# A lambda-layer bottleneck in 32 images: v's transfers on ScalarE's queue, other tiles and copies on VectorE, sums and first outputs in another order

## Chip, cores and metric

One core of a Trainium2 chip runs the whole program. The metric is the device time of one execution in microseconds (us). The engines are TensorE (PE: matrix products), VectorE (DVE), ScalarE (ACT), GpSimd (POOL) and SyncE (SP). Each works through its own instructions in order, and semaphores order them against each other. SP and ACT also issue DMA transfers, from queues of their own. An x of 32 images with 512 channels of 64x64 points comes from DRAM in float32, and the output goes back there.

## What is computed

The reference, cut to what matters, with `x` an image of 512 channels:

```python
n = group_norm(x)                          # 32 groups of 16 channels
h = relu(bn1(conv1x1(n, w1)))              # 512 -> 128 channels
q = bnq(conv1x1(h, wq))                    # 64 = 4 heads x 16
k = softmax(conv1x1(h, wk), axis=channels) # 16
v = bnv(conv1x1(h, wv))                    # 32
pos = conv2d(v, emb, 15x15, "same")        # for each of 16 k and 32 v
content = k @ v.T                          # 16 x 32
lam = q . content + q . pos                # 128 channels
h = relu(bn2(lam))
out = x + relu(bn3(conv1x1(h, w3)) + n)    # 128 -> 512 channels
```

## The kernel before

The image loop is software-pipelined. One trip of it has two stages. The stage `lam` computes image b's lambda from q and v, and takes image b+1's group statistics beside it. The stage `mixed` (the list `MIX`) then works on two images in turn: the last convolution and output of image b, and the projections c (conv1), q and k/v of image b+1. A prologue (`PRO`) and an end (`END`) do the same for the first and the last image. Pixels are cut into four chunks of 1024; `c0` to `c3`, `q0` to `q3` and `k0` to `k3` are the chunks' matmul groups, `o<j>.<t>` is the output tile of chunk j and channel block t (tile n = 4j+t, 128x1024), `nb` a small bias product, `cl` and `cp` the content lambda, `w<u>.<s>` a slot of the convolution's weights (it becomes the moving operand of `lam`), and `r0`, `r1` their rest.

**The order.** TensorE runs `MIX` exactly as `mix_names` lists it. Each group is written into one of four PSUM buffers, ring0 to ring3. The buffer is `n % 4` of a running count (`placed`); o3.t take ring2 and ring3 by turns, and the weights ring0 and ring1. A group waits until the one before it in its buffer has been read out (`take`, `moved`). The other engines go through the same list in order.

**c, q, k.** ACT turns c's PSUM into h1 (L779) and issues the reload of x for the output (L781, its only DMAs). For q, ACT writes a bfloat16 part (L787) and DVE the remainder r1 (L970). For k, DVE copies k out, writes v, takes the maximum and subtracts it (L977 to L983). ACT casts r1 (L791), spreads v over three copies (`spread_v`, L728 to L730) and takes the exponential of k (`softmax_exp`, L720). `softmax_sum` on DVE (L954 to L956) waits for that exponential, sums, takes the reciprocal and multiplies: it normalizes k. In the kernel before it runs for chunk j-1 behind k's work of chunk j, and for chunk 3 right behind that. POOL makes the third part of q (`split_q`, L1164).

**v's way.** After k3, `store_v` writes v to DRAM in three window transfers and a rest (L365, L368), and `load_v` reads it back in the layout of the convolution (L375, L376). Both are issued by SP, in one program with q's stores (L351, L352), q's loads (L358, six a chunk), the output's stores (L400) and the next image's x (L343). `cl` waits for all four normalized chunks (`soft_ready`), `w0.0` for all of q's loads (`q_in`), `lam` for v's.

**Output.** A tile in `VEC_TILES` takes two DVE passes (L1019, L1022). A tile in `POOL_TILES` takes one DVE pass into S (L1015), a ReLU on ACT (L735, `relu_half`, one place later) and an addition on POOL (L1171). `bn2_relu` on ACT (L715) must have made chunk j of h2 before o<j>.<t>.

**The lead.** The first unit of weights, w0.0 to w0.7, r0 and r1, closes `MIX`. `BY_DVE` names the slots that DVE copies out of PSUM (L696 on both engines); ACT copies the rest.

Of the kernel before, what the change touches and what calls it, by code (L numbers as in the profile page):

```python
# [12 lines left out]
P = 128  # L13
# [3 lines left out]
PAD = (R - 1) // 2  # L17
# [10 lines left out]
BLK = 8  # L28
WROWS = 21
WCOLS = 22  # L30
TROWS = 6 * WROWS
# [7 lines left out]

BY_DVE = {0: (1, 5), 1: (1, 3), 2: (3,), 3: (3,), 4: (3,), 5: (1, 3, 5, 7)}  # L40
ACT_SLOTS = [(u, s) for u in range(UNITS) for s in range(NS) if s not in BY_DVE[u]]
# [4 lines left out]

VEC_TILES = [0, 2, 3, 5, 7, 8, 10, 12, 13, 15]
POOL_TILES = [n for n in range(16) if n not in VEC_TILES]
# [12 lines left out]
def mix_names():  # L61
    order = ["c0", "nb", "c1", "q0", "k0", "o0.0", "o0.1", "c2", "q1", "k1", "o0.2", "o0.3", "c3", "q2", "k2", "q3", "k3",
             "o1.0", "o1.1", "o1.2", "o1.3", "cl", "o2.0", "cp", "o2.1", "o2.2", "o2.3"]
    lead = lead_names()
    for t in range(4):
        order += [f"o3.{t}", lead[t]]
    return order + lead[4:]
# [25 lines left out]
def lambda_block(nc, x, w1, bn1, wq, bnq, wk, wv, bnv, emb, bn2, w3, bn3, out):  # L93
# [9 lines left out]
    NCH = N // CHUNK  # L103
# [15 lines left out]
    with ctx:  # L119
# [221 lines left out]
        def _(sp):  # L341
# [18 lines left out]

            def store_v(im):
                sp.wait_ge(vpad_ready, im * 3 + 3)
                sp.wait_ge(vx_ready, im * (3 * NCH) + 3 * NCH)
                for a, n in ((0, 8), (8, 8), (16, 5)):
                    sp.dma_start(vD[PAD:PAD + W, a:a + n, :],  # L365
                                 vX[:, 0:n, a // BLK:a // BLK + NYB, :].rearrange("x r m v -> x r (m v)"))\
                        .then_inc(v_out, 16)
                sp.dma_start(vR[PAD:PAD + W, :], vX[:, 5, 2:2 + NYB, :].rearrange("x m v -> x (m v)"))\  # L368
                    .then_inc(v_out, 16)

            def load_v(im):
                sp.wait_ge(v_out, im * 64 + 64)
                for t in range(3):
                    src = bass.AP(vD.tensor, t * TROWS * ROW, [[ROW, P], [BLK * WROWS * ROW, NXB], [1, ROW]])
                    sp.dma_start(V[:, t, :, :], src).then_inc(v_in[t], 16)  # L375
                sp.dma_start(Vrem, bass.AP(vR.tensor, 0, [[ROW, WCOLS], [BLK * ROW, NXB], [1, ROW]])).then_inc(vrem_in, 16)  # L376

            def load_v3(b):
# [56 lines left out]
            for j in range(NCH):  # L435
                store_q(0, j)
                load_q(0, j)
            store_v(0)
            load_v(0)

# [9 lines left out]
            with nc.Fori(0, B - 1, engines=OrderedEngineSet([sp.engine]), hint_back_edge=True) as b:  # L450
                lam(b, False)
                store_q(b + 1, 0)
                load_q(b + 1, 0)
                store_out(b, 0)
                store_out(b, 1)
                store_q(b + 1, 1)
                load_q(b + 1, 1)
                store_out(b, 2)
                store_q(b + 1, 2)
                store_out(b, 3)  # L460
                load_q(b + 1, 2)
                store_q(b + 1, 3)
                store_v(b + 1)
                load_q(b + 1, 3)
                load_v(b + 1)
                for n in range(4, 16):
                    store_out(b, n)
# [241 lines left out]
        def _(act):  # L709
            def bn2_relu(b, j):  # L710
# [4 lines left out]
                nc.scalar.activation(part, part, ACT.Relu, bias=pbi[:, 1:2], scale=psc[:, 1:2]).then_inc(h2_ready, 1)  # L715

            def softmax_exp(im, j):
                cols = slice(j * (CHUNK // P), (j + 1) * (CHUNK // P))
                act.wait_ge(kmax_done, im * NCH + j + 1)
                nc.scalar.activation(kS[:, cols, :], kS[:, cols, :], ACT.Exp).then_inc(kexp_done, 1)  # L720
# [49 lines left out]
            def front(name, at, im, with_reload):  # L770
# [18 lines left out]
                else:  # L789
                    act.wait_ge(r1_ready, im * NCH + j + 1)  # L790
                    nc.scalar.copy(q12[:, 0, j * CHUNK:(j + 1) * CHUNK], r1[:, j % 2, :]).then_inc(qm_done, 1)  # L791
                    spread_v(im, j)
                    softmax_exp(im, j)

# [15 lines left out]
            act.wait_ge(setup_vd, 8 * 16)  # L810
            for name in PRO:
                if name[0] in "wr":
                    lead(name, AT_PRO, 0)
                elif name[0] in "cqk" and name[1] in "0123":
                    front(name, AT_PRO, 0, False)
            with nc.Fori(0, B - 1, engines=OrderedEngineSet([act.engine]), hint_back_edge=True) as b:
                lam(b, True)
                late = []
                for name in MIX:
# [6 lines left out]
                    late = []  # L826
                    if name == "c0":
                        bn2_relu(b, 0)
                        bn2_relu(b, 1)
                    if name == "k0":  # L830
                        bn2_relu(b, 2)
                        bn2_relu(b, 3)
                    if name[0] == "o" and int(name[1]) * CT + int(name[3:]) in POOL_TILES:
# [10 lines left out]
        def _(dve):  # L844
# [113 lines left out]
            def front(chain, name, at, im):  # L958
                kind, j = name[0], int(name[1])
                src = ring[at[name]]  # L960
                if kind == "q":
                    dve.wait_ge(q_full, im * NCH + j + 1)
                    dve.wait_ge(qh_ready, im * NCH + j + 1)
# [9 lines left out]
                elif kind == "k":  # L973
# [9 lines left out]
                    nc.vector.tensor_tensor(k, k, spread, ALU.subtract).then_inc(kmax_done, 1)  # L983
                    if j:
                        softmax_sum(chain, im, j - 1)

# [243 lines left out]
```

## Time and profile before

| | us |
|---|---|
| median of 3 runs | 5176.27 |
| lowest, highest | 5169.3, 5177.41 |
| the profiled execution | 5191.58 |
| its span, first to last instruction | 5188.9 |

The profile is of one execution. Its page gives each engine's busy time and groups of instructions; further views of the same trace list waits, instructions in order of time, the chain of work that ended last, and stretches with the granted TensorE clock. Times within the trace are from the span's start. Idle time in brackets stands ahead of an instruction, with what released it. All stretches below are of one trip of the loop in the middle of the run, whose `nb` products stand at 2604.07.

### The profile page before, as it was taken

The page shows a single profiled execution, that of the slowest core. Times are in us where ns is not written, and L with a number is a line of the kernel's source. Part 1 is how long each engine was busy: PE and PEld are TensorE (multiplying, and loading weights), DVE is VectorE, ACT ScalarE, POOL GpSimd, SP SyncE. Part 2 cuts the span into 40 slices and gives each one's busy share as a digit, 9 for nine tenths or more (in the row PEclk, how much of TensorE's full clock was granted, in tenths as well). Part 3 has the DMA queues.
Part 4 walks back from the last instruction along what each step waited for, and adds up shares of the span by engine and source line. Part 5 has one row for each costly group of instructions (what it writes and reads, how often), then busy time and mean ns, then how long its engine had stood idle before and what let it go on. Part 6 is the DMA issues. An engine that isn't in the chain of part 4 may idle for free.

```text
span 5188.9 us, 120753 instructions
## 1 busy us (share of the span) xinstructions
PE 4668.3 (90%) x49366; PEld 2754.3 (53%) x49366; DVE 2959.6 (57%) x4695; ACT 2285.5 (44%) x2816; POOL 748.1 (14%) x433
## 2 busy tenths in 40 slices
PE   4989999998999999999989998999988999999997
PEld 2555555554555555555545555555555555555554
DVE  4456555565555565655655555655556565566564
ACT  1444445444444444444444444444444444444443
POOL 0011110111111111101111111111011111111111
PEclk8899999899999989999899989899999999998998
DMA  3678767778777787677787777876777867778776
GB/s 96 224 241 292 261 215 257 245 259 292 231 236 253 252 281 266 217 249 248 257 290 234 232 256 246 287 261 210 256 249 260 289 226 236 248 253 290 254 221 227
DMA packets 537170, 1284.13 MB, mean 247 GB/s; under 512 B 43048, under 2 KB 225324, under 8 KB 528556
## 3 DMA queue, kind: packets, MB, share of 16 engines
q1 hardware_dynamic: 471276, 1017.22, 60.1%
q10 hardware_dynamic: 65472, 260.05, 13.5%
q8 instruction: 415, 6.80, 0.6%
q14 instruction: 7, 0.06, 0.0%
HBM read 844.79 MB, written 432.33 MB: 246 GB/s over the span
## 4 chain that ended last, share of the span: by engine, by line
PE 63%; issue 11%; DVE 9%; DMA 5%; SPq 4%; ACT 4%; POOL 3%; ACTq 0%; DVEq 0%; POOLq 0%
PE ring L522 16%; PE ring L503 14%; PE ring L648 13%; PE ring L578 7%; PE ring L602 4%; DMA X<-x_dram 3%; PE ring L529 3%; POOL X L1171 2%; PE ring L534 2%; PE ring L612 2%; SPq L358 2%; DVE S L1015 2%; ACT region L696 1%; DVE region L696 1%; DMA q_parts<-region 1%
## 5 line engine op out<-in xcount | busy, mean ns | idle before, releaser
L696 ACT COPY region<-ring 126x1024 f32<-126x1024 f32 x1184 | 1163.9, 1016 | 1157.0 <-PE ring L503 1147.8
L578 PE MATMUL ring<-h,w3T 128*128 128x512 f32 x2048 | 1015.6, 639 | 108.4 <-DVE S L1015 76.7
L503 PE MATMUL ring<-Qt,Ep 96*126 96x256 bf16 x5120 | 855.7, 309 | 112.5 <-ACT region L696 62.8
L522 PE MATMUL ring<-X,w1e 128*128 128x512 f32 x2048 | 907.8, 596 | 28.8 <-DVE w1e L892 28.8
L648 PE MATMUL ring<-region,V 126*32 126x128 f32 x24576 | 879.9, 288 | 24.9 <-issue 24.7
L503 PEld LDWEIGHTS ring<-Qt,Ep 96*126 96x126 bf16 x5120 | 628.9, 153 | 358.8 <-issue 181.8
L648 PEld LDWEIGHTS ring<-region,V 126*32 126x32 f32 x24576 | 678.6, 115 | 246.9 <-issue 236.1
L696 DVE COPY region<-ring 126x1024 f32<-126x1024 f32 x352 | 430.3, 1222 | 646.7 <-PE ring L503 646.7
L868 DVE BATCH_NORM_STATS2 st<-X 128x6 f32<-128x512 f32 x1024 | 624.7, 680 | 199.2 <-DMA X<-x_dram 199.1
L578 PEld LDWEIGHTS ring<-h,w3T 128*128 128x128 f32 x2048 | 388.5, 201 | 536.1 <-issue 387.6
L522 PEld LDWEIGHTS ring<-X,w1e 128*128 128x128 f32 x2048 | 385.0, 191 | 496.3 <-issue 493.0
L1171 POOL TENSOR_TENSOR X<-X,S 128x1024 f32<-128x1024 f32 x192 | 451.3, 2351 | 1014.4 <-ACT S L735 1014.4
L970 DVE SCALAR_TENSOR_TENSOR region<-ring,pbi,region 64x512 f32<-64x512 f32 x256 | 179.4, 739 | 708.0 <-ACT region L787 706.9
L1019 DVE SCALAR_TENSOR_TENSOR ring<-X,r1cur,ring 128x1024 f32<-128x1024 f32 x320 | 410.9, 1284 | 138.0 <-PE ring L578 136.9
L735 ACT ACTIVATE S<-S,bcur 128x1024 f32<-128x1024 f32 x192 | 220.1, 1147 | 545.1 <-DVE S L1015 545.1
L1164 POOL TENSOR_TENSOR region<-region 64x1024 bf16<-64x1024 f32 x128 | 272.9, 2132 | 1200.6 <-ACT region L791 1200.6
L779 ACT ACTIVATE region<-ring,nb 128x1024 f32<-128x1024 f32 x128 | 141.9, 1109 | 645.5 <-PE ring L522 344.6
L1022 DVE SCALAR_TENSOR_TENSOR X<-ring,bcur,X 128x1024 f32<-128x1024 f32 x320 | 410.9, 1284 | 11.3
L1157 POOL MEMSET region<- 64x224 f32 x32 | 13.1, 411 | 2220.0 <-PE ring L648 2176.2
L534 PEld LDWEIGHTS ring<-wkvT,region 128*128 128x128 f32 x2048 | 238.2, 191 | 103.9 <-issue 77.9
L534 PE MATMUL ring<-wkvT,region 128*128 128x48 f32 x2048 | 254.1, 277 | 0.0
L1015 DVE SCALAR_TENSOR_TENSOR S<-X,rcur,ring 128x1024 f32<-128x1024 f32 x192 | 244.6, 1274 | 5.5 <-PE ring L578 5.2
(127 smaller groups left out, 2980.1 us busy)
## 6 DMA issues: line engine op xcount, KB each, us to landing
X<-x_dram SPq DMA_DIRECT2D x132, 2048.0 KB, 21.0
out_dram<-X SPq DMA_DIRECT2D x512, 512.0 KB, 9.8
X<-x_dram ACTq DMA_DIRECT2D x124, 2048.0 KB, 9.8
Qt<-q_parts SPq DMA_DIRECT2D x768, 128.0 KB, 3.0
V<-v_windows SPq DMA_DIRECT2D x96, 1024.0 KB, 8.1
lambda_sums<-S SPq DMA_DIRECT2D x64, 1024.0 KB, 3.9
h<-lambda_sums SPq DMA_DIRECT2D x256, 256.0 KB, 5.2
q_parts<-region SPq DMA_DIRECT2D x128, 256.0 KB, 4.1
```

What stands on the lines that cost most here:

```text
L503: last = nc.tensor.matmul(dst[0:TROWS, i * 256:(i + 1) * 256], taps(u, xo, yo), Q[:, :, xo * BLK + yo, :], start=(i % 2 == 0), stop=True, ...
L522: last = nc.tensor.matmul(dst[:, hh * HALF:(hh + 1) * HALF], w1e[:, c, :], X[:, j, c, hh * HALF:(hh + 1) * HALF], start=(c == 0), stop=(c ...
L534: last = nc.tensor.matmul(dst[:, i * KV:(i + 1) * KV], h1[:, j % 2, i * P:(i + 1) * P], wkvT[:, :], start=True, stop=True)
L578: last = nc.tensor.matmul(dst[:, yb * HALF:(yb + 1) * HALF], w3T[:, t, :], src, start=True, stop=True)
L648: last = nc.tensor.matmul(bank_of(i)[c * DV:(c + 1) * DV, (g % 4) * P:(g % 4 + 1) * P], V[0:TROWS, VSLOT[t], xb, yb * DV:(yb + 1) * DV], W ...
L696: return engine_copy(dst, src)
L868: return nc.vector.bn_stats(st[:, c, 2 * j + hh, :], X[:, j, c, hh * HALF:(hh + 1) * HALF])
L1015: nc.vector.scalar_tensor_tensor(T[:, i % 2, :], X[:, j, t, :], rcur[:, t:t + 1], src[:, :], ALU.mult, ALU.add).then_inc(half_sum, 1)
L1019: nc.vector.scalar_tensor_tensor(src[:, :], X[:, j, t, :], r1cur[:, t:t + 1], src[:, :], ALU.mult, ALU.add).then_inc(whole_sum, 1)
L1022: nc.vector.scalar_tensor_tensor(X[:, j, t, :], src[:, :], bcur[:, t:t + 1], X[:, j, t, :], ALU.add, ALU.max).then_inc(out_ready, 1)
L1164: nc.gpsimd.tensor_tensor(q12[:, 1, cols], r1[:, j % 2, :], q12[:, 0, cols], ALU.subtract)\
L1171: nc.gpsimd.tensor_tensor(X[:, j, t, :], X[:, j, t, :], T[:, i % 2, :], ALU.add).then_inc(pool_out, 1)
```

## The change

1. `store_v` and `load_v` move from SP's program to ACT's. The stores are issued in k3's work, between `spread_v` and `softmax_exp`; the loads at o1.2 (in the prologue at w0.0). SP's list closes over the gap, and its output stores come one place later, o1.0 (tile 4) ahead of q's last loads.
2. `VEC_TILES` goes from 10 tiles to 12, so `POOL_TILES` goes from 1, 4, 6, 9, 11, 14 to 5, 7, 9, 11.
3. Of the lead, DVE copies w0.5 and w0.7, where it copied w0.1 and w0.5.
4. `softmax_sum` of chunk j-1 stands ahead of q<j>'s work on DVE, where it stood behind k<j>'s. The last one stays behind k3.
5. o0.0 and o0.1 come behind k1 (before: k0), o0.2 and o0.3 behind c3 (before: k1). `bn2_relu` of the four chunks goes behind k0, k1, q2 and q3 (before: two behind c0, two behind k0).

```diff
-BY_DVE = {0: (1, 5), 1: (1, 3), 2: (3,), 3: (3,), 4: (3,), 5: (1, 3, 5, 7)}
+BY_DVE = {0: (5, 7), 1: (1, 3), 2: (3,), 3: (3,), 4: (3,), 5: (1, 3, 5, 7)}
-VEC_TILES = [0, 2, 3, 5, 7, 8, 10, 12, 13, 15]
+VEC_TILES = [0, 1, 2, 3, 4, 6, 8, 10, 12, 13, 14, 15]
...
-    order = ["c0", "nb", "c1", "q0", "k0", "o0.0", "o0.1", "c2", "q1", "k1", "o0.2", "o0.3", "c3", "q2", "k2", "q3", "k3",
+    order = ["c0", "nb", "c1", "q0", "k0", "c2", "q1", "k1", "o0.0", "o0.1", "c3", "o0.2", "o0.3", "q2", "k2", "q3", "k3",
...
+            def store_v(im):
+                act.wait_ge(vpad_ready, im * 3 + 3)
+                act.wait_ge(vx_ready, im * (3 * NCH) + 3 * NCH)
+                for a, n in ((0, 8), (8, 8), (16, 5)):
+                    act.dma_start(vD[PAD:PAD + W, a:a + n, :],
...
                     spread_v(im, j)
+                    if j == NCH - 1:
+                        store_v(im)
                     softmax_exp(im, j)
...
+                    if name == "o1.2":
+                        load_v(b + 1)
-                    if name == "c0":
+                    if name == "k0":
                         bn2_relu(b, 0)
+                    if name == "k1":
                         bn2_relu(b, 1)
-                    if name == "k0":
+                    if name == "q2":
                         bn2_relu(b, 2)
+                    if name == "q3":
                         bn2_relu(b, 3)
...
                 if kind == "q":
+                    if j:
+                        softmax_sum(chain, im, j - 1)
                     dve.wait_ge(q_full, im * NCH + j + 1)
...
-                    if j:
-                        softmax_sum(chain, im, j - 1)
```

ACT, in the loop, at k3: the cast, the three copies of v and the exponential of the kernel before. In both kernels kS is k, region holds v's copies and q's parts, and S the halves of POOL's tiles.

```order
L791 CAST region<-region 64x1024
L728 COPY region<-region 64x4x64
L729 COPY region<-region 64x3x64
L730 COPY region<-region 64x64
L720 ACTIVATE kS<-kS 128x128
L734 REGISTER_ALU
L735 ACTIVATE S<-S,bcur 128x1024
```

ACT, the same place in the changed kernel.

```order
L788 CAST region<-region 64x1024
L725 COPY region<-region 64x4x64
L726 COPY region<-region 64x3x64
L727 COPY region<-region 64x64
L698 ISA
L699 ISA
L701 DMA v_windows<-region 64x8x256 x2
L701 DMA v_windows<-region 64x5x256
L704 DMA v_rest<-region 64x256
L717 ACTIVATE kS<-kS 128x128
```

Two waits and four transfers now stand between v's copies and k3's exponential, and the exponential's own row is otherwise unchanged.

DVE, in the loop, the end of tile 3 and the start of q2 and k2 in the kernel before (ring3 is tile 3's buffer, ring1 q2's).

```order
L1022 SCALAR_TENSOR_TENSOR X<-ring3,bcur,X 128x1024
L962 REGISTER_ALU
L970 SCALAR_TENSOR_TENSOR region<-ring1,pbi,region 64x64x8 x2
L977 COPY kS<-ring2 128x128
```

DVE, the same place in the changed kernel: tile 3 (ring0), then the sum of chunk 1, then q2.

```order
L1024 SCALAR_TENSOR_TENSOR ring0<-X,r1cur,ring0 128x1024
L1026 REGISTER_ALU
L1027 SCALAR_TENSOR_TENSOR X<-ring0,bcur,X 128x1024
L959 TENSOR_REDUCE kst<-kS 128x8
L859 REGISTER_ALU
L960 RECIPROCAL kst<-kst 128x8
L859 REGISTER_ALU
L961 TENSOR_TENSOR kS<-kS,kst 128x128
L969 REGISTER_ALU
L977 SCALAR_TENSOR_TENSOR region<-ring1,pbi,region 64x64x8 x2
```

The three instructions of chunk 1's sum moved from behind k2 to ahead of q2, and tile 3's two passes come straight before them, since their matmuls moved behind c3.

## Rows read from the trace of the kernel before

**Rows 1.** The page: busy time, share of the span and instructions of each engine.

```profile
PE 4668.3 (90%) x49366; PEld 2754.3 (53%) x49366; DVE 2959.6 (57%) x4695; ACT 2285.5 (44%) x2816; POOL 748.1 (14%) x433
```

**Rows 2.** Waits of PE: who waited for whom, us in total, times, longest.

```profile
PE ring L578 <- DVE S L1015: 76.7, 31, 3.0
PE ring L612 <- issue: 68.8, 35, 2.4
PE ring L554 <- DVE Qt L991: 63.2, 32, 2.0
...
PE ring L648 <- issue: 24.7, 14, 3.4
```

**Rows 3.** PE in order of time: start, us, line, count, [idle before <- releaser].

```profile
2640.22 1.93 PE L529 MATMUL ring<-region,wqT 128*64 128x512 f32 x4
...
2647.68 7.10 PE L578 MATMUL ring<-h,w3T 128*128 128x512 f32 x16
...
2661.78 0.34 PE L554 MATMUL ring<-Qt 16*96 16x32 f32 x2 [2.03 <-DVE Qt L991]
...
2671.34 2.54 PE L578 MATMUL ring<-h,w3T 128*128 128x512 f32 x4 [2.17 <-DVE S L1015]
2675.14 1.11 PE L503 MATMUL ring<-Qt,Ep 96*126 96x256 bf16 x4 [1.25 <-DMA Qt<-q_parts]
2676.04 3.59 PE L578 MATMUL ring<-h,w3T 128*128 128x512 f32 x4
```

**Rows 4.** DVE in order of time, from tile 3 to tile 11.

```profile
2638.16 1.28 DVE L1022 SCALAR_TENSOR_TENSOR X<-ring,bcur,X 128x1024 f32<-128x1024 f32 x1
2643.53 1.40 DVE L970 SCALAR_TENSOR_TENSOR region<-ring,pbi,region 64x512 f32<-64x512 f32 x2 [4.09 <-ACT region L787]
...
2651.58 1.66 DVE L956 TENSOR_TENSOR kS<-kS,kst 128x128 f32<-128x128 f32 x1
...
2653.71 0.29 DVE L956 TENSOR_TENSOR kS<-kS,kst 128x128 f32<-128x128 f32 x1
2653.92 1.27 DVE L1015 SCALAR_TENSOR_TENSOR S<-X,rcur,ring 128x1024 f32<-128x1024 f32 x1
...
2670.01 1.27 DVE L1015 SCALAR_TENSOR_TENSOR S<-X,rcur,ring 128x1024 f32<-128x1024 f32 x1
```

**Rows 5.** ACT at q3 and k3, in order of time.

```profile
2647.08 1.24 ACT L787 ACTIVATE region<-ring,pbi 64x512 bf16<-64x512 f32 x2
2649.84 1.04 ACT L791 CAST region<-region 64x1024 bf16<-64x1024 f32 x1 [1.53 <-DVE region L970]
...
2651.74 0.30 ACT L720 ACTIVATE kS<-kS 128x128 f32<-128x128 f32 x1
```

**Rows 6.** POOL's `split_q` of chunk 3, in order of time.

```profile
2650.96 2.13 POOL L1164 TENSOR_TENSOR region<-region 64x1024 bf16<-64x1024 f32 x1 [2.74 <-ACT region L791]
```

**Rows 7.** SP in order of time: issue start, us, line, what is transferred, count.

```profile
2661.66 3.71 SPq L365 DMA_DIRECT2D v_windows<-region  x3
2665.42 2.50 SPq L368 DMA_DIRECT2D v_rest<-region  x1
2667.97 4.82 SPq L358 DMA_DIRECT2D Qt<-q_parts  x6
```

**Rows 8.** Issues of L365 and L368: ns min/median/max, first and last start.

```profile
L365 SPq DMA_DIRECT2D v_windows<-region x96: 587/660/2389, 138.6 to 5040.6; - x96
...
L368 SPq DMA_DIRECT2D v_rest<-region x32: 2291/2468/2517, 142.1 to 5042.9; - x32
```

**Rows 9.** The chain that ended last, ACT's queue at c2: start, us, what.

```profile
2626.31 0.38 ACTq L781
...
2626.73 0.04 ACTq L734
```

**Rows 10.** Stretches: us, busy (x count) of PE, PEld, DVE, ACT, POOL, granted clock, DMA share, GB/s.

```profile
2550.00:2554.00 4.00, 3.86 (x54) 3.25 (x53) 4.00 (x7) 1.93 (x2) 0.00 (x0) 0.50 1.04 414
...
2674.00:2678.00 4.00, 2.87 (x7) 1.83 (x8) 2.49 (x2) 1.01 (x1) 0.89 (x1) 0.50 0.95 318
```

More of the change, by code:

```diff
@@ L359, in load_q @@
                         .then_inc(q_in[j], 16)
[L361 to L376, printed above, removed]
             def load_v3(b):
@@ L437, in _ @@
                 load_q(0, j)
-            store_v(0)
-            load_v(0)
             def lam(b, last):
@@ L453, in _ @@
                 load_q(b + 1, 0)
+                store_q(b + 1, 1)
+                load_q(b + 1, 1)
                 store_out(b, 0)
                 store_out(b, 1)
-                store_q(b + 1, 1)
-                load_q(b + 1, 1)
+                store_q(b + 1, 2)
                 store_out(b, 2)
-                store_q(b + 1, 2)
                 store_out(b, 3)
@@ L462, in _ @@
                 store_q(b + 1, 3)
-                store_v(b + 1)
+                store_out(b, 4)
                 load_q(b + 1, 3)
-                load_v(b + 1)
-                for n in range(4, 16):
+                for n in range(5, 16):
                     store_out(b, n)
@@ L715, in bn2_relu, with load_v @@
                 nc.scalar.activation(part, part, ACT.Relu, bias=pbi[:, 1:2], scale=psc[:, 1:2]).then_inc(h2_ready, 1)
+            def store_v(im):
[3 more added lines that the diff above has]
+                    act.dma_start(vD[PAD:PAD + W, a:a + n, :],
+                                 vX[:, 0:n, a // BLK:a // BLK + NYB, :].rearrange("x r m v -> x r (m v)"))\
+                        .then_inc(v_out, 16)
+                act.dma_start(vR[PAD:PAD + W, :], vX[:, 5, 2:2 + NYB, :].rearrange("x m v -> x (m v)"))\
+                    .then_inc(v_out, 16)
+            def load_v(im):
+                act.wait_ge(v_out, im * 64 + 64)
+                for t in range(3):
+                    src = bass.AP(vD.tensor, t * TROWS * ROW, [[ROW, P], [BLK * WROWS * ROW, NXB], [1, ROW]])
+                    act.dma_start(V[:, t, :, :], src).then_inc(v_in[t], 16)
+                act.dma_start(Vrem, bass.AP(vR.tensor, 0, [[ROW, WCOLS], [BLK * ROW, NXB], [1, ROW]])).then_inc(vrem_in, 16)
             def softmax_exp(im, j):
@@ L811, in _ @@
             for name in PRO:
+                if name == "w0.0":
+                    load_v(0)
                 if name[0] in "wr":
```

## The prediction, made before the changed kernel was run

> **What bounds the kernel now.** I read the page first, then PE's waits, then one trip of the loop in order of time on PE, DVE, ACT, POOL and SP. PE is busy for 90% of the span, DVE for 57%, ACT for 44% [rows 1]. PE is the bound in most of a trip, and an edit pays only where PE waits. Its largest waits come once a trip (31 times each), for DVE in the middle of `mixed` and for nothing that the profile shows in `lam` [rows 2]. In the trip shown PE works without a gap through c, q, k and o1.0 to o1.3, until 2654.8 [rows 3]. Then it waits for DVE, above all ahead of cp (2.03 us) and of o3.0 (2.17 us, for tile 11's pass to free the buffer) [rows 3]. DVE itself has no real pause from q2's pass at 2643.53 to the end of tile 11's pass at 2671.28 [rows 4]. So this stretch is DVE's, every us of delay in it reaches o3.0, and behind that the lead and `lam`.
>
> **The change, part by part**, for one trip, in the times of that trip.
>
> *Outputs one place later.* PE's work up to o1.3 keeps its sum and has no gap, so q2 still starts at 2640.22 [rows 3]. A full-speed tile takes 7.10/4 = 1.78 us of PE [rows 3], so tile 2's matmuls now end at about 2638.5. DVE's two passes for tiles 2 and 3 (four by 1.28 us) end at 2643.6, where they ended at 2639.44 and left DVE idle for 4.09 us [rows 4]. The cover is gone. With chunk 1's sum (0.8 us) ahead of it, q2's pass starts at 2644.4 and not at 2643.53: +0.9 us. `bn2_relu` sits in ACT's pauses.
>
> *Sums ahead of q.* The multiply of a sum takes 0.29 us alone, but 1.66 where POOL's `split_q` runs, and ends 0.15 us behind POOL [rows 4, 6]. Behind k2 and k3 it met POOL; chunks 0 and 1 now don't. Chunk 2's sum must wait for its exponential, which ACT reaches 0.9 us later than before, right ahead of q3's ACT part [rows 5]. So q3's pass on DVE stays 0.9 us late. Behind k3 there is one sum less on DVE, but the last waits for k3's exponential (now ending 0.95 us later than 2652.04) and then for POOL (3.09 becomes 4.0). It ends at 2654.3, and tile 4's pass begins 0.4 us later than before, if nothing else stands in ACT's way. These two edits together: +0.4 us. Bounds: -0.7 (no delay at q2) to +0.9 (all of it stays).
>
> *v's transfers on ACT.* The stores stand ahead of k3's exponential. SP needs 3.71 us to issue the three window stores and 2.50 for the rest, 6.2 us from 2661.66 to 2667.92 [rows 7]; over the whole run the medians are 0.66 and 2.47 [rows 8]; with two windows at 0.66, the third at 2.2 (here 3.71 less 1.32 is 2.4), the four make 6.0. That this is not SP's backlog alone shows in the least value for the rest, 2291 ns, over all 32 images, the first with its idle queues among them [rows 8]. ACT's own issue of x, 0.38 us, is followed by its next queue instruction only behind its end [rows 9], so I take the exponential to be held for the sum. Bounds: four at the least window value, 0.59, is 2.4 us; with the greatest, 2.39, for each window store and 2.52 for the rest it is 9.7. I take 6.0, since the same four transfers take it on the other queue. The exponential then ends at 2659.0, not 2653.0, and chunk 3's sum (0.8 us, with no `split_q` beside it any more) at 2659.8. Before, tile 4's pass began at 2653.92 [rows 4]. That is +5.9 us, with the delays of the two edits above already in it, and nothing hides it: DVE has tile 4 behind that sum, and cl waits for the sum too. PE has run out of work by 2654.8.
>
> *Tiles.* From tile 4 to tile 11 both kernels have four two-pass tiles and four half tiles (4 and 6 change places with 5 and 7). The 17.4 us from 2653.92 to 2671.28 [rows 4] shrink by the 0.3 us or so that DVE waits for PE in it. In the tail tile 14 takes one more pass, 1.28, and w0.1's copy (1.2) leaves DVE; w0.7's copy joins it, while tile 14's ReLU leaves ACT, where it stood ahead of w0.3's copy. I put the tail at 0, between -0.5 and +1.3. The loads of v on ACT stand ahead of tile 7's ReLU (5.7 us of issue, about 2661 to 2667), whose result POOL and DVE need by tile 11 at 2675: covered by some 5 us.
>
> *SP without v.* q's last loads came behind v's stores [rows 7] and held w0.0 for 1.25 us [rows 3]; they now land well before w0.0. The output stores go out earlier as well, and the next x with them, so the 16 DMA engines, at a share of 1.0 and above through the start of `lam` [rows 10], finish earlier against PE. The wait at L648 with no cause in the profile (24.7 us over the run [rows 2]) came at the end of that full stretch in part of the images. I take -1.0 us for both. Bounds: 0, and -6, if the wait at L612 (2.2 us a trip [rows 2]) and the slow clock behind it also went.
>
> The Trainium skill says of this (DMA: Bandwidth & Descriptors, section "Issuing engines are not separate DMA queues") that transfers from several engines share the same 16 DMA engines, and that a second issuer saves only issue time, "usually small relative to the DMA itself". The first half speaks against a gain in bandwidth; the second doesn't fit v's rest, with 2.47 us of issue for 64 KB.
>
> *The clock.* At 0.50 of the clock (1.2 GHz) a tile's matmuls take 3.59 us, not 1.78 [rows 3, 10]. That stretch came behind the waits ahead of o3.0. Now PE idles some 6 us longer from 2654.8, so I expect more time at 1.2 GHz in o2 and o3. DVE needs 5.1 us for tiles 9 to 11, PE 10.7 for three at 1.2 GHz: if all three fall in it, the trip loses about 3.5 us more, with o3.0 and o3.1 too about 8. If none do, 0. I take +1.5, nearer to none, since PE idles in this stretch anyway.
>
> **Sum.** A trip: 5.9 + 1.5 - 1.0 - 0.3 = +6.1 us; 31 trips: +189. The prologue hides the stores (w0.0 waits there for q's loads), and in the end DVE has two more passes of 1.28, with POOL's last one gone: +2. Together +191. The profiled execution would go from 5191.6 to 5383. The median before is 15 us below it, and the change falls on it alike: 5176.3 + 191 = 5367 us, 3.7% slower.
>
> **The rivals.**
> *The issue is cheap on ACT.* Its queue is idle by then, and 0.38 us for x of 2 MB speaks for it; the least value of the rest, 2.29, against. At 2.4 us for the four, the last sum ends at 2656.2: a trip is 2.3 + 0.5 for the clock - 1.3 = +1.5; 31 by 1.5 + 2 = +49, 5225 us. Chance 0.12.
> *The exponential isn't held (ends faster).* If ACT can start it while the issues run, only +0.4 is left, against -1.0 for SP and DMA, -0.3 for DVE's waits and -0.4 for the clock: -1.3 a trip, 31 by -1.3 + 2 = -38, 5138 us. The point is whether an ACT instruction can begin during an issue that stands ahead of it. No row shows one that does [rows 9]. Chance 0.07. Here the Trainium skill has a rule (Advanced Engine Details and Errata, "Sequencer Loop"): while a control instruction executes, other engine instructions can be read and queued. If issues count as such, this rival holds; no row here shows it.
> *The waits in `lam` go.* With x landing earlier against PE, L612's wait and its slow stretch fall away: -5 a trip more than the forecast, 31 by 1.1 + 2: 5212 us. For it: the wait comes only once a trip, at one place, with the DMA engines full. Against: the DMA traffic still follows tile 15 and reaches over that place. Chance 0.06.
> *The clock falls through o3.* 3.5 to 7 us more a trip than the forecast: 31 by 9.6 + 2 is 5476 us, 31 by 13.1 + 2 is 5584. Chance 0.07.
>
> **Chances.** Forecast 0.66; the rest as above, and 0.02 for no difference. The forecast's own spread is that of the issue (4.5 to 7) and of the clock (0 to 3.5): 31 by 3.1 to 31 by 9.1, 5274 to 5460 us. The range reaches from the cheap issue to there: 5225 to 5460. A difference under about 0.2% (10 us) can't be told from none. Faster 0.08, within it 0.04, slower 0.88.
>
> **What would show it.** ACT: four issues of together about 6 us between v's last copy and k3's exponential. DVE: an idle time of about 7 us (k3's work ends at 2651.9) ahead of the last sum (L959), put down to ACT's exponential. PE: a wait of about 7 us ahead of cl (its buffer is tile 4's, whose two passes end at 2662.3), none for q's loads. The sums' multiplies of chunks 0 and 1 at 0.29 us. o3.0 some 73 us behind `nb`, not 67. The prediction is wrong if that idle time isn't there, or if `lam` becomes shorter by several us.

## The result: 7.1% slower, about twice the loss forecast

| | before | changed |
|---|---|---|
| median, us | 5175.89 | 5539.74 (4 runs, 5528.28 to 5555.31) |
| ratio, 95% interval | 1 | 1.0708 [1.0679, 1.0736] |
| span of the profiled execution | 5188.9 | 5541.3 |
| mean granted clock of TensorE | 0.923 | 0.891 |
| one trip, mean of 31 (`nb` to `nb`) | 157.9 | 168.9 |

The forecast was 5367 us, in a range of 5225 to 5460. The direction was right. The time lies 173 us above the forecast and 80 above the range. A trip became 10.9 us longer, where +6.1 was forecast. 31 trips make 339 of the 352 us by which the span grew.

The page of the changed kernel, which answers to [rows 1], has the same matmuls in a longer span. PE's busy time grew by 40 us, so most of the loss is idle time. In its chain of work the bare "issue" has 13% and ACT's queue 4%:

```profile
PE 4708.6 (85%) x49366; PEld 2811.2 (51%) x49366; DVE 2931.6 (53%) x4759; ACT 2221.8 (40%) x2752; POOL 597.1 (11%) x369
...
PE 61%; DVE 13%; issue 13%; ACT 5%; ACTq 4%; POOL 3%; SPq 1%; DMA 0%; DVEq 0%; POOLq 0%
```

Waits of the changed kernel on PE, DVE and ACT (who waited for whom, us in total, times, longest), against [rows 2]. L530 is cl, L558 the output convolution, L592 the wait in `lam` that stood at L612:

```profile
PE ring L530 <- DVE X L1027: 262.2, 31, 8.6
PE ring L558 <- DVE S L1020: 214.5, 31, 10.2
PE ring L592 <- issue: 92.0, 40, 4.1
...
DVE kst L959 <- ACT kS L717: 354.0, 97, 7.9
...
DVE S L1020 <- POOL X L1176: 114.4, 27, 6.9
...
ACT S L732 <- issue: 322.7, 28, 14.1
...
ACT kS L717 <- issue: 211.9, 32, 6.8
```

There are two new stalls, one in every trip and one in 27 of the 31, and each can be followed through the engines. The first is the one forecast: the exponential (L717) is held for 6.6 us a time, DVE's last sum waits for it, and PE's cl waits 8.5 us for tile 4's passes. The second isn't in the forecast: a ReLU (L732) is held for 11.5 us a time (28 times), POOL's addition (L1176) waits for that, DVE's pass of tile 11 (L1020) for POOL, and PE's o3.0 for DVE, 6.9 us a trip where [rows 2] has 2.5.

ACT in one trip (its `nb` stands at 2599.82), in order of time, against [rows 5]. L701 and L704 are v's stores, L711 and L712 v's loads:

```profile
2648.60 4.24 ACTq L701 DMA_DIRECT2D v_windows<-region  x3
2652.87 2.32 ACTq L704 DMA_DIRECT2D v_rest<-region  x1
2655.24 0.31 ACT L717 ACTIVATE kS<-kS 128x128 f32<-128x128 f32 x1 [6.67 <-issue]
2660.17 1.15 ACT L732 ACTIVATE S<-S,bcur 128x1024 f32<-128x1024 f32 x1 [4.63 <-DVE S L1020]
2660.25 6.88 ACTq L711 DMA_DIRECT2D V<-v_windows  x3
2667.16 8.16 ACTq L712 DMA_DIRECT2D Qt<-v_rest  x1
2675.44 2.19 ACT L732 ACTIVATE S<-S,bcur 128x1024 f32<-128x1024 f32 x2 [14.12 <-issue]
```

The row at 2655.24 is the forecast's first step. The last three rows are the step that failed: the loads' issue takes 15.0 us here, and the ReLUs of tiles 7 and 9 come together behind it. The same place on DVE, POOL and PE, against [rows 4] and [rows 3]:

```profile
2655.58 0.29 DVE L959 TENSOR_REDUCE kst<-kS 128x8 f32<-128x128 f32 x1 [7.73 <-ACT kS L717]
...
2656.14 0.29 DVE L961 TENSOR_TENSOR kS<-kS,kst 128x128 f32<-128x128 f32 x1
...
2670.84 1.28 DVE L1027 SCALAR_TENSOR_TENSOR X<-ring,bcur,X 128x1024 f32<-128x1024 f32 x1
2679.04 1.28 DVE L1020 SCALAR_TENSOR_TENSOR S<-X,rcur,ring 128x1024 f32<-128x1024 f32 x1 [6.92 <-POOL X L1176]
```

```profile
2676.66 4.66 POOL L1176 TENSOR_TENSOR X<-X,S 128x1024 f32<-128x1024 f32 x2 [12.84 <-ACT S L732]
```

```profile
2659.01 3.59 PE L530 MATMUL ring<-region,kS 128*16 128x32 f32 x64 [8.48 <-DVE X L1027]
...
2680.38 3.37 PE L558 MATMUL ring<-h,w3T 128*128 128x512 f32 x4 [10.15 <-DVE S L1020]
```

The margin can be read off these rows. DVE was free for tile 11 at 2672.1. To have tile 7's half out of S by then, POOL (2.35 us) had to begin at 2669.8 and the ReLU (1.15) at 2668.6. The loads began at 2660.25. So a string of issues of up to 8.3 us costs nothing here, and the string of 15.0 us came 6.8 us too late for that; DVE waited 6.92.

SP at the same time, against [rows 7], and then the group of all its issues of q's loads (min/median/max in ns). The six loads of q's chunk 2 take 1.5 us each beside ACT's stores, where the median over the run is 0.6:

```profile
2648.99 9.01 SPq L358 DMA_DIRECT2D Qt<-q_parts  x6
...
L358 SPq DMA_DIRECT2D Qt<-q_parts x768: 578/597/2312, 105.8 to 5388.2; - x192
```

Over all trips the stores' issue takes 6.5 us and the loads' 12.2 (the mean, from 60.4 to 72.7 us behind `nb`). The groups of the loads' issues (min/median/max in ns) are of that size by their medians, 3 by 1.98 and 7.37, together 13.3:

```profile
L711 ACTq DMA_DIRECT2D V<-v_windows x96: 387/1984/4601, 137.0 to 5384.2; - x96
...
L712 ACTq DMA_DIRECT2D Qt<-v_rest x32: 2375/7368/8521, 140.5 to 5387.4; - x32
```

### The profile page after: what moved, and what is told of

Read it like the earlier page. It is cut to its first block, busy times and chain, and to the rows that moved or that the text cites. A ratio compares the mean times of both kernels' runs of the same rounds, so it can differ in the third digit from the quotient of the medians.

```text
span 5541.3 us, 120502 instructions
## 1 busy us (share of the span) xinstructions
PE 4708.6 (85%) x49366; PEld 2811.2 (51%) x49366; DVE 2931.6 (53%) x4759; ACT 2221.8 (40%) x2752; POOL 597.1 (11%) x369
## 4 chain that ended last, share of the span: by engine, by line
PE 61%; DVE 13%; issue 13%; ACT 5%; ACTq 4%; POOL 3%; SPq 1%; DMA 0%; DVEq 0%; POOLq 0%
PE ring L502 16%; PE ring L483 14%; PE ring L628 13%; PE ring L558 6%; DVE ring L1024 5%; PE ring L582 4%; POOL X L1176 2%; ACTq L701 2%; PE ring L514 2%; PE ring L509 2%; PE ring L592 2%; DVE S L1020 1%; DVE region L676 1%; ACTq L704 1%; DVE region L977 1%
## 5 line engine op out<-in xcount | busy, mean ns | idle before, releaser
L558 PE MATMUL ring<-h,w3T 128*128 128x512 f32 x2048 | 1022.0, 642 | 232.4 <-DVE S L1020 214.5
L558 PEld LDWEIGHTS ring<-h,w3T 128*128 128x128 f32 x2048 | 396.6, 205 | 673.4 <-issue 398.5
L1024 DVE SCALAR_TENSOR_TENSOR ring<-X,r1cur,ring 128x1024 f32<-128x1024 f32 x384 | 492.9, 1284 | 320.2 <-PE ring L558 319.5
L1027 DVE SCALAR_TENSOR_TENSOR X<-ring,bcur,X 128x1024 f32<-128x1024 f32 x384 | 493.1, 1284 | 13.7
L1176 POOL TENSOR_TENSOR X<-X,S 128x1024 f32<-128x1024 f32 x128 | 299.6, 2350 | 798.2 <-ACT S L732 798.2
L732 ACT ACTIVATE S<-S,bcur 128x1024 f32<-128x1024 f32 x128 | 143.8, 1144 | 601.1 <-issue 322.7
L530 PE MATMUL ring<-region,kS 128*16 128x32 f32 x2048 | 113.2, 240 | 273.5 <-DVE X L1027 262.2
L530 PEld LDWEIGHTS ring<-region,kS 128*16 128x16 f32 x2048 | 108.3, 129 | 299.3 <-DVE X L1027 287.9
```

Source lines behind the costliest of these rows:

```text
L558: last = nc.tensor.matmul(dst[:, yb * HALF:(yb + 1) * HALF], w3T[:, t, :], src, start=True, stop=True)
L1024: nc.vector.scalar_tensor_tensor(src[:, :], X[:, j, t, :], r1cur[:, t:t + 1], src[:, :], ALU.mult, ALU.add).then_inc(whole_sum, 1)
L1027: nc.vector.scalar_tensor_tensor(X[:, j, t, :], src[:, :], bcur[:, t:t + 1], X[:, j, t, :], ALU.add, ALU.max).then_inc(out_ready, 1)
L1176: nc.gpsimd.tensor_tensor(X[:, j, t, :], X[:, j, t, :], T[:, i % 2, :], ALU.add).then_inc(pool_out, 1)
```

## The experiments

The kernels start from the changed one, but for the one headed as part 1 alone. Ratios are against the kernel before, run beside it on the same chip. A trip is the mean from `nb` to `nb` over 31 stretches, of which the first holds the end of the prologue in place of a `mixed`. Each is read from one profiled execution, so differences of a few tenths are not told from none.

### v's transfers back on SP

Parts 2 to 5 are left as they are; only part 1 is undone. In the diff the lines taken out are ACT's, the ones put in SP's.

```diff
-                    if j == NCH - 1:
-                        store_v(im)
...
-                    if name == "o1.2":
-                        load_v(b + 1)
...
                 store_q(b + 1, 3)
-                store_out(b, 4)
+                store_v(b + 1)
                 load_q(b + 1, 3)
+                load_v(b + 1)
+                store_out(b, 4)
```

> The changed kernel with v's stores and loads issued by SP again, at the places of the kernel before (stores ahead of q's last loads, loads behind them); tiles, lead copies, sums and output order stay changed. Theory A (all the loss comes from ACT's two strings of issues, the stores ahead of k3's exponential and the loads ahead of tile 7's ReLU): within 20 us of the kernel before, 5176. Theory B (the output order, the two more double-pass tiles and DVE's copies of w0.5 and w0.7 carry a good part): 5250 or more.

Measured: 5160.67 us, ratio 0.9992 [0.9975, 1.0008], a trip of 157.1 us: theory A. The whole loss goes with part 1. Parts 2 to 5 neither cost nor gain by themselves: cl now waits 2.0 us (0.5 before) and o3.0 3.2 (2.5 before), cp a little less, and the mean clock is 0.936.

### One of the two holds at a time

The stores are put behind the exponential (loads still on ACT, ahead of tile 7's ReLU):

```diff
                     spread_v(im, j)
+                    softmax_exp(im, j)
                     if j == NCH - 1:
                         store_v(im)
-                    softmax_exp(im, j)
```

> The changed kernel with ACT issuing v's stores behind k3's exponential and not ahead of it. The loads stay at o1.2, ahead of tile 7's ReLU. Theory A1 (the two holds add up: 6 us for the stores, 4 to 5 for the loads): 6 us a trip less, about 5350. Theory A2 (they overlap, since the loads can't start before the stores have landed, some 60 us behind nb, and then hold tile 7's ReLU, and through POOL DVE's tile 11, until about 73 us behind nb whatever came before): only about 1 us a trip less, 5500 to 5530, with DVE's wait ahead of the last sum gone and its wait for POOL at tile 11 longer by as much.

Measured: 5528.02 us, ratio 1.071 [1.068, 1.0739], a trip of 168.1: theory A2. The wait at cl fell to 2.0 us, and next to none of it was gained. Waits of PE, DVE and ACT in this kernel:

```profile
PE ring L558 <- DVE S L1020: 427.8, 31, 17.2
...
PE ring L530 <- DVE X L1027: 63.1, 31, 2.0
...
DVE S L1020 <- POOL X L1176: 331.5, 31, 14.1
...
ACT S L732 <- issue: 696.1, 62, 19.1
```

o3.0 now waits 13.8 us a time: what cl waits less is there. Its time is set by the loads, and these can't start earlier: they wait for v's stores to land, some 60 us behind `nb` in both kernels.

The loads leave ACT for SP, behind q's last loads (stores still ahead of the exponential):

```diff
-                    if name == "o1.2":
-                        load_v(b + 1)
...
                 load_q(b + 1, 3)
+                load_v(b + 1)
```

> The changed kernel with v's loads issued by SP behind q's last loads; the stores stay on ACT ahead of k3's exponential. Theory A (the loads' issue on ACT is what the forecast had too small): the wait of DVE for POOL at tile 11 goes, the wait ahead of the last sum (7.7 us) stays: about 4.5 us a trip less than the changed kernel, 5380 to 5420, where the forecast of 5367 would have been near. Theory C (the excess is the clock: the 8 us of idle PE ahead of cl bring 1.2 GHz into o2 and o3): less than 1.5 us a trip back, 5490 or more.

Measured: 5414.08 us, ratio 1.0489 [1.0463, 1.0515], a trip of 164.7: theory A. Only the forecast's stall is left. L539 is cl here, L567 the output convolution, L957 DVE's sum, L719 the exponential. The page's first line, and waits:

```profile
PE 4674.6 (86%) x49366; PEld 2790.9 (52%) x49366; DVE 2929.4 (54%) x4759; ACT 2224.3 (41%) x2752; POOL 597.8 (11%) x369
...
PE ring L539 <- DVE X L1025: 260.4, 31, 8.7
...
PE ring L567 <- DVE S L1018: 97.6, 31, 3.2
...
DVE kst L957 <- ACT kS L719: 352.4, 97, 7.9
...
ACT kS L719 <- issue: 210.2, 32, 6.9
```

Both edits together:

> Both: ACT issues v's stores behind k3's exponential, SP issues v's loads behind q's last loads. Theory A: neither hold is left, so near the kernel before or below it, 5130 to 5190, since SP no longer spends 6 us on the stores ahead of q's last loads. Theory B (the other parts cost): 5250 or more.

Measured: 5169.55 us, ratio 0.9996 [0.9978, 1.0015], a trip of 157.2: theory A. ACT still issues the stores here, behind the exponential, and the ReLU behind them starts late (200.3 us over 31 times in this kernel's row of waits), but nobody waits for that. The page's first line, and waits:

```profile
PE 4592.8 (89%) x49366; PEld 2720.8 (53%) x49366; DVE 2946.8 (57%) x4759; ACT 2222.1 (43%) x2752; POOL 596.7 (12%) x369
...
PE ring L567 <- DVE S L1018: 101.2, 31, 3.7
PE ring L601 <- issue: 90.8, 49, 2.4
PE ring L539 <- DVE X L1025: 63.0, 31, 2.0
...
PE ring L637 <- issue: 40.5, 17, 4.4
...
ACT S L734 <- issue: 200.3, 31, 6.8
```

The four kernels make a square (us a trip):

| | loads on SP | loads on ACT |
|---|---|---|
| stores behind the exponential | 157.2 | 168.1 |
| stores ahead of it | 164.7 | 168.9 |

Stores alone +7.5, loads alone +10.9, both +11.7. The delays of the two holds run beside each other and end at the same place, o3.0, so they don't add.

### Part 1 alone, on the kernel before

> The kernel before with v's stores and loads issued by ACT, at the changed kernel's places; nothing else changed. Theory A (the two holds on ACT are the whole loss, about 11.5 us a trip by the runs with v on SP): 5500 to 5560. Theory B (the holds cost less without the changed tiles and order, since the output order or tile 7's place makes them bite): under 5450.

Measured: 5413.95 us, ratio 1.0473 [1.0447, 1.0498], a trip of 164.8, +6.8. Theory A of that text missed and B held. The loads take 7.8 us there, not 12.2, DVE waits next to nothing for POOL (3.7 us over the whole run, 114.4 in the changed kernel), and cl waits 5.3 us, not 8.5. So part 1 costs 6.8 us a trip on the kernel before, and 11.8 (168.9 less 157.1) on top of parts 2 to 5, though these cost nothing by themselves. What of them does it is the question of the last two experiments.

### The loads behind tile 7's ReLU

The stores are behind the exponential, and the loads come at cl, behind the ReLU that they held:

```diff
-                    if name == "o1.2":
+                    if name == "cl":
                         load_v(b + 1)
```

> The changed kernel with ACT's stores behind k3's exponential and ACT's loads at cl, behind tile 7's ReLU and not ahead of it; both strings of issues still run on ACT. Theory A (the loads cost through that one ReLU: POOL's addition of tile 7 is late, and DVE's pass for tile 11 waits for the buffer): against 5528 with the loads ahead of the ReLU some 9 to 11 us a trip come back, 5170 to 5240; what stays is that w0.0's and w0.1's copies wait for the end of the issues, about 74 us behind nb. Theory D (a string of 12 to 15 us of issues on ACT costs its length wherever it stands in mixed): 5400 or more.

Measured: 5387.09 us, ratio 1.043 [1.0408, 1.0451], a trip of 163.9, against 168.1 with the loads one place earlier: between the two theories. The stall at o3.0 went to 3.3 us, which shows that it was this one ReLU. But another stall came up, in all trips. PE's waits:

```profile
PE ring L483 <- DMA Qt<-q_parts: 168.0, 32, 17.7
...
PE ring L558 <- DVE S L1020: 103.6, 31, 3.6
```

w0.0 waits 4.9 us a trip for q's last loads, which land some 74 us behind `nb`, while v's loads are under way on the other queue. Slow issue on SP isn't the reason: these six loads take 3.9 us to issue, 3.8 with neither hold (means over the trips). But the last of them lands 6.6 us behind its issue, where it takes 2.3 with neither hold. So the time is lost behind the issue; whether to v's loads or to the output stores beside them isn't separated.

### SP kept quiet while ACT issues the loads

SP issues q's last loads only once most of V has landed:

```diff
                 store_out(b, 4)
+                sp.wait_ge(v_in[2], b * 16 + 32)
                 load_q(b + 1, 3)
```

> The changed kernel, and SP waits for the third of v's window loads to land before it issues q's last loads and the output stores behind them, so that ACT issues v's loads while SP issues nothing. It measures a duration, the time gets worse (w0.0 waits for q). Theory G (SP's issues and transfers beside it stretch ACT's string for v's loads, 12.2 us in the changed kernel against 5.6 on SP before): the string falls to 6 to 9 us. Theory H (ACT's queue issues these loads slower by itself): it stays at 11 or more.

Measured: 5599.43 us, ratio 1.0827 [1.0775, 1.0878], a trip of 170.4, since w0.0 now waits 4.5 us for q. What it was made for is the issue: the loads' string takes 8.2 us a trip, where it took 12.2, and the rest of v 2.7 us, where it took 6.7. That is theory G, but not the whole of the growth: the three window loads take 5.6 us here and 5.5 in the changed kernel, and 2.7 on SP in the kernel before. No run tells what makes the windows longer on ACT, so theory H isn't excluded for them. One trip of this kernel, ACT in order of time, and PE's waits:

```profile
2686.62 5.50 ACTq L712 DMA_DIRECT2D V<-v_windows  x3
2692.15 2.84 ACTq L713 DMA_DIRECT2D Qt<-v_rest  x1
2695.10 1.15 ACT L733 ACTIVATE S<-S,bcur 128x1024 f32<-128x1024 f32 x1 [7.41 <-issue]
```

```profile
PE ring L531 <- DVE X L1028: 261.2, 31, 8.7
PE ring L484 <- DMA Qt<-q_parts: 152.1, 32, 11.8
PE ring L559 <- DVE S L1021: 104.2, 31, 5.1
```

At 8.3 us in this trip the string is right at the margin worked out above, and the stall at o3.0 is 3.4 us a trip, as without any loads on ACT.

### The order of the outputs undone

Parts 1 to 4 stay; the order of part 5 is that of before again, and with it `bn2_relu`'s places and SP's list (the diff is cut to the order).

```diff
-    order = ["c0", "nb", "c1", "q0", "k0", "c2", "q1", "k1", "o0.0", "o0.1", "c3", "o0.2", "o0.3", "q2", "k2", "q3", "k3",
+    order = ["c0", "nb", "c1", "q0", "k0", "o0.0", "o0.1", "c2", "q1", "k1", "o0.2", "o0.3", "c3", "q2", "k2", "q3", "k3",
```

> The changed kernel with the output order, bn2's places and SP's order as before (v's transfers on ACT at the changed kernel's places, tiles, lead copies and sums changed). With v's transfers alone moved the loss was 7.7 us a trip, with all parts 11. Theory G (the changed order lets SP's q loads and ACT's v issues run at the same time, which stretches ACT's string; with it undone v's loads end about 66 us behind nb and tile 7's ReLU no longer holds DVE's tile 11): 5380 to 5440. Theory I (the changed tiles do it: POOL's tile 7 is the second of four, and its buffer is wanted by tile 11): 5500 or more.

Measured: 5424.07 us, ratio 1.0503 [1.0456, 1.0549], a trip of 164.1: theory G by the time. The profiled execution is the fastest of four, 34 us under their median, or 1.1 us a trip. PE's wait at o3.0 (L558), and the groups of the loads' issues on ACT:

```profile
PE ring L558 <- DVE S L1018: 124.6, 31, 7.3
```

```profile
L711 ACTq DMA_DIRECT2D V<-v_windows x96: 387/1256/4785, 136.4 to 5234.5; - x96
...
L712 ACTq DMA_DIRECT2D Qt<-v_rest x32: 1311/3700/8625, 140.2 to 5235.9; - x32
```

The stores' string takes 5.6 us (6.5 in the changed kernel), the loads' 8.2 (12.2), and they start 2 us earlier, 58.5 us behind `nb`. The second stall is all but gone: DVE waits for POOL in 6 trips, 14.1 us in all, where it was 114.4. So the order, free by itself, makes ACT's strings longer.

How it does that is shown in part. The stores' string and the loads of q's chunk 2, issued together, are both shorter here: 5.6 us against 6.5, and 7.0 against 9.1. For v's loads the overlap alone doesn't tell the two kernels apart: q's last loads fall under them in both, and take 4.0 and 4.1 us to issue. They begin 0.2 us ahead of v's rest here, and 2.2 us ahead of it in the changed kernel (medians). Within the changed kernel, v's rest takes 4.0 us in the 7 trips in which they begin less than 1.5 us ahead of it, and 7.5 us in the other 24; with the stores behind the exponential that split is small (6.7 and 7.2). SP's list was changed along with the order, and no run separates the two.

### Two trials at the waits in `lam`, and one at the tiles

All three have neither hold (stores behind the exponential, loads on SP). In the first, chunks 2 and 3 of the next image's x are issued behind unit 2's weights:

```diff
-                    for j in range(NCH):
+                    for j in range(2):
...
+                    sp.wait_ge(w_full, b * (UNITS * NS) + 3 * NS)
+                    for j in range(2, NCH):
```

> The version with neither hold, and in it SP issues chunks 2 and 3 of the next image's x only after the weights of unit 3 have begun (about 106 us behind nb), so that the DMA engines aren't full when PE reaches L592's place in lam. It tests the forecast's rival on lam. Theory E (PE's wait of 2.0 us there, for no cause in the profile, and the 1.2 GHz behind it come from instructions fetched late while the DMA engines are full): the wait and most of the slow clock behind it go, 2 to 5 us a trip, 5010 to 5110, unless x now comes too late for the statistics. Theory F (the wait has nothing to do with the x traffic): wait unchanged, 5150 or more.

Measured: 5207.01 us, ratio 1.008 [1.0054, 1.0105], a trip of 158.4: theory F. The wait some 105 us behind `nb` stayed (2.8 us). The one at 120 us went, and in its place PE waits 44.2 us over the run for DVE (L699), whose statistics wait longer for x (229.8 us over the run, 156.6 with x on time).

In the second, three quarters of the next image's x are left out (one channel block of four is loaded):

```diff
-                        load_x(b + 1, j)
+                        sp.dma_start(X[:, j, 0:1, :], xv[b + 1, :, 0:1, j * CHUNK:(j + 1) * CHUNK])...
```

> The version with neither hold, and in the loop SP loads only one of the four channel blocks of the next image's x (0.5 MB a chunk, not 2), so that the DMA engines fall idle early in lam. The other three blocks of the loop's images keep what is in the buffer, so the output is that of other inputs; the work of all engines is the same. It does what the late loads of x could not: take the traffic away from under PE's wait of 2.0 us in lam (105 us behind nb). Theory E (instructions fetched late while the DMA engines are full): the wait goes or falls under 0.5 us, the later waits without a cause too, and the 1.2 GHz behind them; 4 to 8 us a trip less than 5170, 4920 to 5050. Theory F: the wait stays at 2.0 us, 5130 or more.

Measured: 5143.42 us, ratio 0.995 [0.993, 0.9969], a trip of 156.2. PE's longest wait in it:

```profile
PE ring L601 <- issue: 103.1, 31, 5.1
```

The later waits (L637: 40.5 us with all of x) are gone. The first one, L601, even grew, from 2.0 us a trip to 3.3. So x's traffic is not its cause, and theory E falls for it. All such waits together went from 131.3 to 103.1 us over the run, 0.9 us a trip, which is nearly the whole gain of 1.0.

In the third, tile 4 is POOL's again and w0.7's copy ACT's, to take work off DVE ahead of cl:

```diff
-BY_DVE = {0: (5, 7), ...
+BY_DVE = {0: (5,), ...
-VEC_TILES = [0, 1, 2, 3, 4, 6, 8, 10, 12, 13, 14, 15]
+VEC_TILES = [0, 1, 2, 3, 5, 7, 8, 10, 12, 13, 14, 15]
```

> The version with neither hold (stores on ACT behind the exponential, loads on SP), and in it POOL's tiles 4, 6, 9, 11 in place of 5, 7, 9, 11, and ACT copying all of the lead but w0.5. Theory A (DVE's chain from q2 to tile 11 has a fixed length, and only PE's wait ahead of cl and the copies in the lead change): cl's wait goes from 2.0 to 0.5 us and moves to o2.0 and cp, the lead gets 0.3 to 0.7 us shorter: 5140 to 5165. A rival: w0.7's copy on ACT stands behind w0.6's and gives the time back: 5160 to 5185.

Measured: 5177.97 us, ratio 1.002 [1.0006, 1.0033], a trip of 157.1: the rival's time, not theory A's. cl's wait went from 2.0 to 0.8 us and came back, mostly at cp (2.0). No kernel run here that loads all of x is clearly faster than the kernel before; those with neither hold and nothing else changed are equal to it.

## Why the prediction was right, and where it failed

| us a trip | forecast | measured | from |
|---|---|---|---|
| stores ahead of the exponential, with the clock behind it | 5.9 + 1.5 = 7.4 | 7.5 | 164.7 less 157.2 |
| SP without v, DVE's shorter waits, tail, order | -1.0 - 0.3 + 0 = -1.3 | -0.7 | 157.2 less 157.9 |
| loads ahead of tile 7's ReLU | 0 | +4.2 | 168.9 less 164.7 |
| sum | +6.1 | +10.9 (rounded terms) | 168.9 less 157.9 |

The measured -0.7 is no gain that could be told from none: the profiled execution of the kernel before lies 16 us above its median, 0.5 us a trip, and the ratio of the kernel with neither hold is 0.9996. Of what the prediction's -1.0 was made of, the wait for q's loads went in the loop, but the wait without a cause at L648 didn't: with neither hold it is 40.5 us over the run (L637), 24.7 before.

**The stores' hold: right.** The string was put at 6.0 us and took 6.5 (6.56 in the trip shown), the exponential starts only behind it, the multiply of the last sum takes 0.29 us with no `split_q` beside it, and the sum ends at 2656.4, 56.6 us behind `nb` (forecast 2659.8, 55.7 behind it). cl waits 8.5 us (about 7 forecast). With the loads on SP, o3.0's matmuls stand 73.8 us behind `nb` ("some 73").

**The rival "the exponential isn't held": refuted.** The row at 2655.24 shows 6.67 us of idle time put down to issue, and the run has 32 such waits. A DMA issue occupies ACT for the instructions behind it: in the changed kernel ACT has 224 issues longer than 0.5 us, and none of its instructions begins inside one. An instruction ahead of an issue can still run beside it, as the ReLU at 2660.17 does. The rule of the Trainium skill that the prediction weighed (Advanced Engine Details and Errata, "Sequencer Loop") says only that other instructions can be read and queued meanwhile; reading ahead isn't seen in the trace, and it gave no earlier start here.

**The rival "the issue is cheap on ACT": refuted.** The store of v's rest takes 2.27 to 2.63 us to issue on ACT's queue, 2.29 to 2.52 on SP's [rows 8].

**The loads' term: the step that failed.** The prediction put the loads at 5.7 us of issue, called them "covered by some 5 us", and so put their term at nothing; it measured +4.2 us a trip. Two numbers in it were off. The spare was smaller: from the loads' start to tile 11's pass it took 14 us, the trace shows 11.9, so strings up to 8.3 us are covered, 2.6 more than 5.7. And above all the string takes 12.2 us. The prediction shows no row for the 5.7, but the trace bears it out for SP: in the kernel before, SP issues these four transfers in 5.8 us (mean; 5.4 to 7.4), 2.7 for the windows and 3.1 for the rest, and ACT issues nothing beside them. In the changed kernel ACT issues them while SP issues q's last loads and output stores. Of the 6.4 us more, 4.0 go when SP is kept quiet, all of them in v's rest (6.7 to 2.7); the windows stay 2.9 us longer than on SP, and the cause of that is open. The string is 8.2 us with SP quiet, 8.2 with the old order, 7.8 with part 1 alone, and in each DVE waits only 4 to 14 us over the whole run for tile 11's buffer, not 114. For the stores the prediction had given bounds of 2.4 to 9.7 us; for the loads it gave none, and with that no range for the term that it set to nothing. The same spread for the loads (5.7 times 9.7/6.0 is 9.2) would have gone over the real edge of 8.3, but not over the 10.7 (5.7 and 5) that the prediction took it to be. So both had to be known, the length and the spare.

**How the terms add.** The prediction summed its terms. For the holds the square shows that this would be wrong: the loads' hold costs 10.9 us a trip alone, but 4.2 on top of the stores'. If the stores' hold had been found first and mended alone, next to nothing would have been gained (168.9 to 168.1).

**The clock.** It is inside the 7.5. Between the two kernels behind it PE's wait at cl grows by 6.4 us, and o3.0 comes 6.8 later. PE's idle time grows by 5.1 us a trip in all, since some waits behind cl shrink, and the other 2.4 are work at a slower clock (1.5 forecast). The pages agree: PE's busy time for the same products is 4674.6 us against 4592.8, 2.6 a trip. In the trip shown cl's 64 products take 3.59 us right behind the 8.48 us wait, where with a 2.03 us wait ahead they take 2.04 in a trip of the kernel with the loads behind tile 7's ReLU; over all trips the means are 3.5 us with the stores' hold and 2.6 with neither. The granted clock of that trip of the changed kernel, in the stretches of cl, of o3.0, and of o3.1 to o3.3 (columns as in [rows 10]):

```profile
2659.00:2662.60 3.60, 3.60 (x65) 3.51 (x65) 3.56 (x4) 1.15 (x1) 1.13 (x1) 0.50 0.95 253
...
2680.30:2683.80 3.50, 3.42 (x6) 1.58 (x7) 0.04 (x2) 1.15 (x1) 3.24 (x2) 0.58 1.02 405
2683.80:2692.00 8.20, 7.83 (x32) 4.07 (x30) 8.09 (x7) 3.61 (x4) 0.13 (x1) 1.00 0.66 268
```

So of o3 only the first tile is slow (3.65 us in the mean over the trips; the other three take 1.9 to 2.1), and the clock didn't fall through o3. That rival (5476 to 5584 us) holds the measured time by its number alone; its mechanism isn't what happened.

**The smaller steps.** w0.0's wait for q's loads went, as forecast. The wait in `lam` (L592) stayed, so "the waits in `lam` go" is refuted. The prologue was put at 0 ("the prologue hides the stores"), and costs 5.5 us from the first `nb` to the second, 144.3 against 138.8. cl waits 11.3 us there for the last sum (6.2 before), and behind it w0.0 12.6 for q's loads (7.4 before): SP issues the last of them 5 us later, since those ahead of them take 8.07 us beside ACT's stores and not 3.78. With the stores behind the exponential and the loads on SP the stretch is still 143.2, and 139.5 with all of v on SP, so most of it is that longer issue and not the hold. The 2 us forecast for the end aren't there: from the last product of `lam` to the end of the program both kernels take 54.9 us. What follows the last `nb` grew by 13, 11.3 of it up to o3.0 of the last `mixed`.

## What to carry to other kernels

A DMA issue on a compute engine is to be charged at its place in that engine's order, like an instruction of its length: look who needs the next result of that engine, and how much spare time there is to the point where the chain comes back to the bound. The length has to be taken under the conditions of the new place, with another queue issuing at the same time, or carried with bounds: one read where only one queue was issuing was half of what it became. The spare wants the same care: both are read at the new place. Delays that run beside each other to the same end don't add; what each costs is seen only by taking away each alone and both.

## What the runs showed of the hardware

**Issues on two queues at once take longer, and not evenly.** SP's six loads of one chunk of q in the prologue, in the kernel before and then in the changed kernel, where ACT issues v's stores (3.50 and 2.38 us) at the same time:

```profile
126.86 3.78 SPq L358 DMA_DIRECT2D Qt<-q_parts  x6
```

```profile
127.01 8.07 SPq L358 DMA_DIRECT2D Qt<-q_parts  x6
```

The Trainium skill (DMA: Bandwidth & Descriptors, "Issuing engines are not separate DMA queues") says that a second issuer saves issue time only. Here it saved little even of that: ACT took over 5.9 us of issue, and SP's 3.78 became 8.07, 4.3 more. In the loop the same pair costs SP 5.3 us (9.1 against 3.8, by the kernel with v on SP) and ACT some 0.5 (6.5 against the 6.0 that SP needed for the stores). With q's last loads beside v's loads it is the other way: SP takes 4.1 us against 3.8, and ACT 6.7 for v's rest against 2.7 with SP quiet. Keeping SP quiet took its transfers away along with its issues, so no run tells whether the issues hold each other up or wait for the transfers under way.

**PE's wait in `lam` is not the traffic's.** It stands once an image at the same place of the program in every kernel, 1.9 to 3.4 us long in the mean, with all of x and with a quarter of it. In all 13 kernels the last 16 KB packet of the queue that loads instructions starts 2.3 to 3.1 us before PE goes on, however long the wait was: with a quarter of x the waits are 0.9 to 5.1 us long, and the packet is 2.3 to 3.1 us back in each. So the end of the wait goes with that packet, and its length with when the packet comes. That it is the cause, and what would bring it earlier, was not tested.
